# Attention on one core: GpSimd adds the absolute values of two neighbouring key blocks before the denominators, and the tables of places in a turn change with it

## The reference, cut to what matters

```python
qr = theta_shift(q, sin_q, cos_q)
kr = theta_shift(k, sin_k[None, None], cos_k[None, None])
qk = jnp.einsum('bhqd,bhkd->bhqk', qr, kr) * mask[None]
den = jnp.clip(jax.lax.stop_gradient(jnp.abs(qk)).sum(-1, keepdims=True), 1.0, 50000.0)
qk = qk / den
out = jnp.einsum('bhqk,bhkd->bhqd', qk, vr).transpose(0, 2, 1, 3)
mu = out.mean(-1, keepdims=True)
var = out.var(-1, keepdims=True)
out = (out - mu) / jnp.sqrt(var + LN_EPS) * ln_g + ln_b
out = jax.nn.gelu(out.reshape(B, L, H * HD), approximate=False)
out = out @ Wo.T
```

## Time and profile before

| | before |
|---|---|
| median of 3 runs | 5166.29 us (5162.64 to 5168.21) |
| time of the profiled execution | 5180.98 us |
| its span | 5179.2 us |
| busy TensorE | 3729.6 us (72%) |
| busy VectorE | 3039.0 us (59%) |
| busy ScalarE | 1464.2 us (28%) |
| busy GpSimd | 1114.0 us (22%) |
| mean granted TensorE clock | 0.843 |

### The profile page before, as it was taken

The page is one execution under the profiler, slowest core; times in us unless marked ns, Lnnn a source line. Parts: engine busy times, 40 slices in busy tenths (PEclk is TensorE's granted clock), DMA queues, the critical chain, the costliest instruction groups (busy, mean ns, idle before and its releaser), DMA issues. The chain is left out here.

```text
span 5179.2 us, 54486 instructions
## 1 busy us (share of the span) xinstructions
PE 3729.6 (72%) x18868; PEld 2091.1 (40%) x18868; DVE 3039.0 (59%) x5760; ACT 1464.2 (28%) x2015; POOL 1114.0 (22%) x1134
## 2 busy tenths in 40 slices
PE   6999999999488367852594774848856775269377
PEld 2333333333355135631362553635524553146244
DVE  3666666666888356887002187688746698501137
ACT  2555555555242012220131221224201121024031
POOL 1111111111001531017204201000163103710610
PEclk9999999999689678875796996868978887689688
DMA  2000000000520000011111372252000001111137
GB/s 115 9 26 25 25 25 17 9 25 17 184 96 34 5 17 26 30 31 12 27 46 39 114 273 92 65 184 96 35 5 25 27 29 26 11 31 63 21 114 284
DMA packets 157191, 302.39 MB, mean 58 GB/s; under 512 B 32132, under 2 KB 115460, under 8 KB 151812
## 3 DMA queue, kind: packets, MB, share of 16 engines
q1 hardware_dynamic: 98244, 181.17, 9.7%
q10 hardware_dynamic: 25920, 94.38, 4.9%
q0 software_dynamic: 32768, 23.36, 2.4%
HBM read 183.47 MB, written 115.35 MB: 58 GB/s over the span
## 5 line engine op out<-in xcount | busy, mean ns | idle before, releaser
L1120 PE MATMUL l_pu<-l_tt,l_w 128*128 128x512 f32 x2048 | 1071.9, 650 | 443.7 <-ACT l_hid L1283 251.8
L1131 PE MATMUL l_pd<-l_w,l_hid 128*128 128x256 f32 x4096 | 984.7, 385 | 97.0 <-issue 70.3
L1131 PEld LDWEIGHTS l_pd<-l_w,l_hid 128*128 128x128 f32 x4096 | 796.3, 195 | 439.8 <-issue 337.8
L1283 ACT ACTIVATE l_hid<-l_pu,l_b 128x512 f32<-128x512 f32 x512 | 349.0, 686 | 1918.8 <-PE l_pu L1120 1318.3
L1120 PEld LDWEIGHTS l_pu<-l_tt,l_w 128*128 128x128 f32 x2048 | 420.1, 209 | 783.8 <-issue 700.5
L370 DVE TENSOR_TENSOR at_pr<-at_ps,at_decay 128x1024 f32<-128x1024 f32 x512 | 604.2, 1218 | 199.7 <-PE at_ps L491 198.5
L298 ACT ACTIVATE at_ab<-at_pr 128x1024 f32<-128x1024 f32 x512 | 537.0, 1055 | 525.2 <-DVE at_pr L370 502.9
L1060 POOL DMA_INDIRECT l_g<-hs_rows,l_i_src x336 | 317.2, 944 | 574.7 <-DVE l_i_src L1714 465.2
L1005 POOL DMA_INDIRECT slots<-l_list,l_to x288 | 280.2, 973 | 320.6 <-DVE l_to L1595 234.7
L491 PE MATMUL at_ps<-at_qr,at_kr 32*128 32x512 f32 x2048 | 318.6, 643 | 22.8 <-DVE at_pr L370 11.8
L1585 DVE TENSOR_TENSOR l_base<-l_base,l_pr 128x128 f32<-128x128 f32 x128 | 36.2, 283 | 431.4 <-remote 304.3
(11 more groups left out here) (336 smaller groups left out, 4446.2 us busy)
## 6 DMA issues: line engine op xcount, KB each, us to landing
ys<-l_yst ACTq DMA_DIRECT2D x112, 512.0 KB
l_yb<-ys SPq DMA_DIRECT2D x28, 2048.0 KB, 9.7
l_tt<-tT ACTq DMA_DIRECT2D x36, 512.0 KB, 3.2
at_xt<-in_x SPq DMA_DIRECT2D x16, 1024.0 KB, 5.5
l_xt<-x SPq DMA_DIRECT2D x32, 512.0 KB, 4.0
tT<-l_xnT ACTq DMA_DIRECT2D x32, 512.0 KB, 4.1
l_xo<-x SPq DMA_DIRECT2D x28, 512.0 KB, 4.1
x<-at_xt SPq DMA_DIRECT2D x8, 1024.0 KB, 4.3
```

What stands on the lines that cost most here:

```text
L1120: ins = pe.matmul(ps_u[q % 2][:, :], w1[:, e, c, P * q:P * q + P], tt[:, s, c, :], start=(c == 0), stop=(c == KK - 1))
L1131: ins = pe.matmul(out, hid[:, k % 2, c, P * r:P * r + P], w2[:, k % GE, c, :], start=False, stop=(c == MB - 1), skip_group_check=True)
L1283: act.activation(hid[:, k % 2, q, :], ps_u[q % 2][:, :], ACT.Gelu, bias=b1[:, k % GE, q:q + 1]).then_inc(s_act, 1)
```

## The change

Three things change in attention.

- GpSimd adds the absolute values of block 2k + 1 to those of block 2k (`pair_sums`, one add for each of the two tiles of a block), and TensorE sums them over keys once for the pair (`denominators(k)` behind the scores of every second block). `ab` has six tiles instead of four, picked by `size`: even blocks alternate between two pairs of tiles, odd blocks share one.
- The rotation factors `t1`, `t2` are kept once instead of twice, so `rotate` waits for the `rotated` before it. `squares` works in place in `dn`, `pq` is gone, and `clip` waits for the variance matmul of the group before.
- The tables move: the last variance, the spread and the output products two blocks later, the variances of groups 0 and 1, the transposes, statistics and normalisation two or three blocks later, `PROJ_A` two, `VALUES` one or none. Clip comes in the fourth block of a group instead of the second.

```diff
-VAR_LAST = 2
-SPREAD = 5
-OUT = {7: 0, 9: 1}
+VAR_LAST = 4
+SPREAD = 7
+OUT = {9: 0, 11: 1}
...
-VAR = {12: 0, 23: 1, 30: 2}
-TRANS = {19: 0, 20: 1}
-PROJ_A = {21: 0, 22: 1, 24: 2, 25: 3}
-VALUES = {27: 0, 29: 1}
+VAR = {15: 0, 25: 1, 30: 2}
+TRANS = {21: 0, 22: 1}
+PROJ_A = {23: 0, 24: 1, 26: 2, 27: 3}
+VALUES = {28: 0, 29: 1}
+NPAIR = NQ // 2
...
+        def size(u, p):
+
+            return ab[:, 2 * (0, 1, 2, 1)[u % 4] + p, :, :]
...
-                    pool.tensor_tensor(pq[:, :], dn[:, :], dn[:, :], ALU.mult).then_inc(s_sqr, 1)
+                    pool.tensor_tensor(dn[:, :], dn[:, :], dn[:, :], ALU.mult).then_inc(s_sqr, 1)
                     pool.wait_ge(s_sqr, at(NGR, n))
-                    pool.tensor_tensor(pq[:, :], pq[:, :], sq[:, :], ALU.add).then_inc(s_pq, 1)
...
+                    pool.tensor_tensor(dn[:, :], dn[:, :], sq[:, :], ALU.add).then_inc(s_pq, 1)
+
+                def pair_sums(k):
+                    for p in range(2):
+                        pool.wait_ge(s_a, at(2 * NQ, 4 * k + 3 + p))
+                        pool.tensor_tensor(size(2 * k, p), size(2 * k, p), size(2 * k + 1, p), ALU.add).then_inc(s_sum, 1)
...
+                    if main and u % 2:
+                        pair_sums(u // 2)
...
-                    if b > 0 or n >= 4:
-                        act.wait_ge(s_den, at(NQ, n // 2 - 1))
-                    act.activation(ab[:, n % 4, :, :], pr[:, n % 4, :, :], ACT.Abs).then_inc(s_a, 1)
+                    k = n // 4
+                    if n // 2 % 2 and (b > 0 or k > 0):
+                        act.wait_ge(s_sum, at(NQ, 2 * k - 1 + n % 2))
+                    if n // 2 % 2 == 0 and (b > 0 or k > 1):
+                        act.wait_ge(s_den, at(NPAIR, k - 1))
+                    act.activation(size(n // 2, n % 2), pr[:, n % 4, :, :], ACT.Abs).then_inc(s_a, 1)
...
-                    if main and u >= 2:
-                        denominators(u - 2)
-                    if tail and u < 2:
-                        denominators(NQ + u - 2, back=1)
+                    if main and u % 2 == 0 and u >= 4:
+                        denominators(u // 2 - 2)
+                    if tail and u in (0, 2):
+                        denominators(NPAIR + u // 2 - 2, back=1)
```

More of the change, by code:

```diff
@@ L151, in attention_layer @@
         s_proj, s_rot, s_vps, s_vc = (sem(k) for k in ("proj", "rot", "vps", "vc"))
-        s_sc, s_a, s_av, s_den = (sem(k) for k in ("sc", "a", "av", "den"))
+        s_sc, s_a, s_av, s_den, s_sum = (sem(k) for k in ("sc", "a", "av", "den", "sum"))
         s_o, s_dn, s_sqr, s_pq, s_var, s_rsd, s_bc, s_g, s_op = (
@@ new lines, in pair_sums @@
+                def pair_sums(k):
+                    for p in range(2):
+                        pool.wait_ge(s_a, at(2 * NQ, 4 * k + 3 + p))
+                        pool.tensor_tensor(size(2 * k, p), size(2 * k, p), size(2 * k + 1, p), ALU.add).then_inc(s_sum, 1)
+                for u in range(NQ):
+                    if main and u == 0:
+                        for i in range(2):
+                            pool.wait_ge(s_ring[slot("v", i, 1)], drained("v", i, 1))
+                        if tail:
+                            pool.wait_ge(s_av, at(NQ, 0))
+                        pool.sem_inc(s_go_p, 1)
+                        pool.tensor_copy(v[:, :, P:C], vs[:, :, :]).then_inc(s_vc, 1)
+                    if main and u - 1 in PROJ_B:
+                        rotated("pB", 1, PROJ_B[u - 1])
+                    if head and u - 1 in PROJ_A:
+                        rotated("pA", 0, PROJ_A[u - 1])
+                    if u % 8 == 3 and (main if u > 3 else tail):
+                        if u > 3:
+                            squares(u // 8 - 1)
+                        else:
+                            squares(3, back=1)
+                    if head and u == 18:
+                        pool.wait_ge(s_ve, at(1, 2))
+                        pool.tensor_tensor(rstd[:, :], ve[:, :], nhalf[:, :], ALU.pow).then_inc(s_rstd, 1)
+                    if main and u % 2:
+                        pair_sums(u // 2)
@@ L448, in turn @@
                         weigh(2 * u)
-                    if u % 8 == 1 and (main if u > 1 else tail):
+                    if u % 8 == 3 and (main if u > 3 else tail):
                         clip(u)
@@ L513, in outputs, with denominators @@
                     ins.then_inc(s_av, 1)
-                def denominators(u, back=0):
-                    hq, qn, kb = quad(u)
-                    if kb == 0 and (b > 0 or u > 0):
-                        pe.wait_ge(s_dn, at(NGR, u // 8))
-                    pe.wait_ge(s_a, at(2 * NQ, 2 * u + 2 - 2 * NQ * back))
+                def denominators(k, back=0):
+                    i = k % (NPAIR // NGR)
+                    if i == 0 and (b > 0 or k > 0):
+                        pe.wait_ge(s_dn, at(NGR, k // (NPAIR // NGR)))
+                    pe.wait_ge(s_sum, at(NQ, 2 * k + 2 - NQ * back))
                     for j in range(HPQ):
-                        ins = pe.matmul(ps_dn[KD * j:KD * j + KD, :], roots[:, :], ab[:, (2 * u + j // 2) % 4, j % 2, :],
-                                        start=(kb == 0), stop=(kb == 7), tile_position=(0, KD * j), skip_group_check=True)
+                        ins = pe.matmul(ps_dn[KD * j:KD * j + KD, :], roots[:, :], size(2 * k, j // 2)[:, j % 2, :],
+                                        start=(i == 0), stop=(i == NPAIR // NGR - 1), tile_position=(0, KD * j), skip_group_check=True)
                     ins.then_inc(s_den, 1)
@@ L545, in variance @@
                     pe.wait_ge(s_ring[slot("var", g)], free("var", g))
-                    pe.matmul(ps[slot("var", g)][KD * g:KD * g + KD, 0, :], blk[:, :], pq[:, :], start=True, stop=True,
+                    pe.matmul(ps[slot("var", g)][KD * g:KD * g + KD, 0, :], blk[:, :], dn[:, :], start=True, stop=True,
                               tile_position=(0, KD * g), skip_group_check=True).then_inc(s_var, 1)
```

33 lines of the change are left out of this document (15 added, 18 removed).

## The result

The changed kernel takes **5202.25 us** (median of 4 runs, 5196.68 to 5204.77) against 5166.2 of the kernel before in the same series: a ratio of 1.0064, 95% interval 1.0044 to 1.0084, so 0.6% slower. The profiled execution took 5202.82 us with a span of 5201.1 us, 21.9 more than before.

The account below looks back on a forecast made before the run. TensorE was taken to bound attention. Per turn -14.1 (denominators) +5.9 (bank pairs) +11.0 (normalisations) = +2.8 us; six turns 17, first 0, last +2, end +4: +22 or so, written 5166 + 20 = 5186 us, range 5115 to 5215.

Parts of the forecast that it names:

- The terms of my sum: All of attention: six turns 17 us, first turn 0, last turn +2, end +4; written as +22 or so.
- 14.7 us above the median: Kernel before: profiled time 5180.98 against median 5166.29; the prediction assumed this difference carries over.
- 10 to 13: Block 11's projection plus output product delay block 12's scores; with block 14's half, +2.9 us a turn.
- A: Normalisations: each L428 waits for one GpSimd instruction; stretch loses 15.4 us, 5186 in all; chance 0.5.
- B: Normalisations: GpSimd keeps the port through back-to-back adds; stretch loses 3.5 to 4 more, 5214; chance 0.15.
- C: Normalisations: L428 gets through as today, fewer than three of eight meet an add; loss about 6, 5120; chance 0.2.
- I walked six of eight L433 into a GpSimd instruction: Normalisation walk: first three end at 20.25, next waits to 25.1, last two end at 30.65 and 33.1; loss 11.45.
- 2.5 to 3: Normalisation stretch: TensorE's clock at the lower level for longer, 2.5 to 3 us of the 15.4.
- the 3.7 of my walk: Blocks 4 to 9: VectorE's reciprocals, spread and split scores lose 3.7 us where today's turn loses 2.1: +1.6.
- Rival D: Bank pairs: losses stay away because TensorE's queue reaches past a waiting half; 5 us a turn less, 5146; chance 0.15.
- 0.5 and 0.85: Bank pairs: split scores from block 1 to 2 cost +0.5; waiting for the second product after block 25, +0.85.
- would lose 2.2%: Denominators issued once for two blocks save 14.1 us a turn, 113 over 8 turns, without any new wait.

Follow-up runs that it names:

- runs 9 to 12: Runs on a third chip; the last two repeat both kernels unchanged: changed kernel 4331.29 us against 4307.0 for the kernel before.
- run 9: Changed kernel with normalisations gathered in block 19 and third rotation in block 12, but GpSimd's adds not held back: 4328.85 us, ratio 1.0055.
- run 3: Kernel before with only the new tables of places, statistics and normalisations, no GpSimd adds: 5191.52 us, ratio 1.0037 to the kernel before.
- run 1: Changed kernel with GpSimd only signalling instead of adding, so denominators omit odd key blocks: 5151.92 us, ratio 0.9962 to the kernel before.
- run 5: Changed kernel with normalisations gathered in block 19, GpSimd's adds held back behind them, and third rotation in block 12: 4268.68 us, ratio 0.9915.
- run 2: Changed kernel with the third rotation (projection) behind block 12 instead of 11: 5162.87 us, ratio 0.9969 to the kernel before.
- run 11: Changed kernel again, unaltered, on a third chip: 4331.29 us against 4307.0 for the kernel before, ratio 1.0057.
- run 4: Changed kernel with all eight normalisations in block 19, GpSimd's adds held back, second group's squares a block later: 5167.85 us, ratio 0.9989.
- run 12: Kernel before again, unaltered, with a profile on the same third chip: 4300.81 us in its one run.

## Why the prediction was right

It said 5186 us, slower, range 5115 to 5215. Measured was 5202, slower: +36 us by the medians, +22 by the profiled executions, +24 by the medians of runs 9 to 12, where +20 was forecast. (The terms of my sum add up to 23; I wrote 22 and used 20.) I let the profiled execution's 14.7 us above the median carry over; the changed kernel's profiled execution was no such outlier, and that is most of the 16 us missing from my number. But a right sum can hide wrong terms, and here it does: that it came within 2 us of the profiled difference is in good part luck, since one stretch came out 2.0 us a turn dearer than forecast and another 3.9 cheaper. The table takes turns 1 to 5 of both traces, and for each stretch of blocks the distance of the first scores less what TensorE's groups take there undisturbed (scores 1.07, denominators 0.88, outputs 0.97, projections 3.63, and so on). What is left is loss, in us a turn:

| blocks | before | after | predicted change | measured change |
|---|---|---|---|---|
| denominators halved, 16 x 0.88 | | | -14.1 | -14.1 |
| 31 and 0 | 2.6 | 3.2 | 0 | +0.6 |
| 1 to 9 | 2.3 | 6.4 | +2.1 | +4.1 |
| 10 to 13 | 0.0 | 3.75 | +2.9 | +3.7 |
| 14 to 22 | 4.55 | 11.6 | +11.0 | +7.1 |
| 23 to 30 | 0.0 | 1.2 | +0.85 | +1.2 |
| a turn | 9.4 | 26.2 | +2.8 | +2.6 |

Copy to copy the same turns grew by 2.2 on the mean. Over the whole of attention: start +3.1 (predicted 0), first turn -0.9 (0), six turns +13.1 (+17), last turn and end +6.7 (+6).

- **Right: the mechanism of A, against B.** One GpSimd instruction for each L433; run 9 shows it five times in a row. C, "fewer than three of eight L428 meet an add", came half true in the changed kernel: two meet an add and two a square or its sum, because the later adds run late. The loss came out between the two prices: 15.4 by A, about 6 by C, 11.6 measured. The rule of the Trainium skill (SBUF — State Buffer, Who interferes with whom) that the shared pair is held for a whole instruction agrees with 2.1 and 2.4 us waits on 2.4 us adds; who gets it next it leaves to the order of issue, and the runs show that to be the other engine, if it waits.
- **Its size was too large.** I walked six of eight L433 into a GpSimd instruction; four met one, as the timeline shows. VectorE was held up, so Abs was, so GpSimd stood idle (3.39 us): the wait limits itself. The eight take 9.2 us a turn after, 4.95 before, 3.2 when free. Against that stands `ve`, 1.2 us that I left out: a small tensor_scalar waits for the port like a large one. The runs split the loss of the stretch: 4.6 us a turn before, 3.5 with the new tables (run 3), 7.2 with the denominators halved as well (run 1), 11.6 with the adds. So the adds are worth 4.4 there. Another 3.8 is the shorter blocks, in which TensorE meets the pace of VectorE.
- **The clock** in that stretch: outputs, scores and transposes between 626.61 and 632.31 take twice their time, 2.7 us that nothing hides; I had 2.5 to 3. What I did not see is that in the changed kernel the clock is low behind block 12's wait as well, +1.6.
- **Blocks 4 to 9 were under-priced.** Blocks 6 to 8 lose 0.53, 2.09 and 1.11 where the clock stays up, together the 3.7 of my walk. But I took 2.1 off for what the kernel before loses there, and it loses 1.1. The other 1.2 of its 2.3 stand in block 2, where TensorE waits for the squares ahead of the last variance matmul, and the new tables remove them: blocks 1 to 3 lose 1.2 before and 0.65 after, where I had added 0.5. Block 9 loses 1.34 more, and ScalarE, which I had not walked, ends last there. From run 5:

```profile
545.59 1.28 ACT L339 ACT_TABLE_LOAD   x1
...
546.88 2.37 ACT L339 ACTIVATE at_xn<-at_xn,at_gb 128x1024 f32<-128x1024 f32 x2
...
549.16 1.04 ACT L305 ACTIVATE at_ab<-at_pr 128x1024 f32<-128x1024 f32 x1
...
550.23 0.60 ACT L313 ACTIVATE at_o<-at_ps_av 128x512 f32<-128x512 f32 x1
...
550.88 1.06 PE L517 MATMUL at_ps_av<-at_pr,at_v 128*32 128x512 f32 x8 [1.25 <-ACT at_o L313]
```

  A table load, two Gelu and an Abs stand ahead of the copy that frees the outputs' bank, and in the new tables all fall before block 8's outputs. The remaining 0.65 is clock.
- **Rival D is out.** Blocks 2 and 26 of the changed kernel lose 0.59 and 0.82 where 0.5 and 0.85 were forecast; TensorE's queue did not reach past the waiting half.
- **Halving the denominators was never worth 113 us.** Even without adds and without the double block it brings 40.6. Blocks 14 to 22 lose 8.1 us in that version and 3.7 in the one with tables alone: of the 3.5 us that the four missing denominators took there, none comes back. VectorE has work without a gap in that stretch, so a shorter block only makes TensorE wait. The same in blocks 4 to 9 (5.1 and 2.4). The prediction had this in its walk, as losses; its first sum, "would lose 2.2%", reads as if it were on offer.

What made the kernel slower is settled by taking it away: block 11's double load is worth 30.8 us by itself, the port 25.0, both together 61.0 (1317.2 to 1256.2), their sum within the scatter. With them gone the change is a gain of 33 to 39 us. The later first copy belongs to the tables; which entry, no run shows.

## What to carry to other kernels

When a short instruction on one engine shares a port with long ones on another, count how often it will meet one, then gather the short ones and hold the long ones back with one wait: the gathering alone made it worse (attention ended at 1313.1 with it and at 1286.4 without). When places in a table move to suit a new operation, run the table by itself; here one entry cost 31 us, and the whole change, with that entry and the port put right, brings 33 to 39. Time taken off one engine comes back only where no other engine sets the pace: of the 113 us taken off TensorE, 41 came back in the version without adds. And walk every engine that frees a buffer, the ones with half their time idle too, before you trust a sum.

## What the hardware showed beside that

- The clock falls behind some waits and not behind others: attention ran at the lower level, 1.2 GHz, for 112.6 us in the changed kernel (139.9 in run 11, the same kernel), 55 in run 5, which does the same work, and 27 in run 3. Behind TensorE's wait of 1.45 us in the rows of run 2 denominators take 1.7 us by starts instead of 0.88; behind 2.06 us in the rows of after scores, outputs and transposes take twice their time. Behind the 1.46 us in the rows of run 3 denominators take 0.89. Shorter waits alone do not keep the clock up either: in run 4 attention is 25 us shorter and at the lower level for 119.5 us.
- The add of two SBUF tiles takes 2.38 us on GpSimd; I had taken 2.44, between bounds of 1.04 and 2.52.
- The activation table load in the rows above takes 1.28 us, and the next activation starts 0.01 us behind it. The Trainium skill (ScalarE: Activation LUTs, What ACT_TABLE_LOAD costs) adds a drain of 1.38 us to that; this trace shows none.
- The part behind attention, untouched, takes 3884 us in the first traces and 3009.8 in run 12, on another chip. The waits of ScalarE there are one difference; first the kernel before in its first trace, then in run 12 (us in total, times, longest):

```profile
ACT l_hid L1283 <- PE l_pu L1120: 1318.3, 325, 83.4
ACT l_hid L1283 <- remote: 562.7, 31, 36.6
```
```profile
ACT l_hid L1283 <- PE l_pu L1120: 1226.6, 361, 46.3
```

  Thirty-one waits of up to 37 us for something outside the core's records are gone in run 12. What they wait for, no trace here shows.
